# A decoder kernel: the last batch's block feed-forward and second norm spread over ten passes of the second self-attention

## What is computed

```python
# x = x + _L0_ffn_ref(_layernorm(x), weight, bias, delta_w, delta_act)      (the block feed-forward)
xb = x.reshape(-1, 32)                          # blocks of 32
amax = max(abs(xb)); e = floor(log2(max(amax, TINY)))
scale = exp2(e - 2.0) * exp2(0.5 * tanh(4 * delta))
xs = xb / scale
q = sign(xs) * _fp4_round(clip(abs(xs), 0.0, 6.0))
y = scale * q;  out = y @ w_q.T + bias

# x = x + _L1_attn_ref(_layernorm(x), ...)                                   (the second self-attention)
q, k, v = split(x @ W_attn.T + b_attn)          # 16 heads of 16 columns
att = q @ k.T / sqrt(16) + rel_bias;  att = softmax(where(causal, att, -inf))
y = (att @ v) @ W_proj.T + b_proj
```

## Time and profile before

| | us |
|---|---|
| median of 3 runs | 1368.73 (1368.17 to 1368.84) |
| the profiled execution | 1369.26 |
| its span, at a mean granted clock of 0.972 | 1367.5 |
| TensorE busy in the span | 1242.6 (91%) |
| VectorE busy | 1004.1 (73%) |
| ScalarE busy | 771.3 (56%) |
| GpSimd busy | 250.3 (18%) |
| the loop of the second self-attention | 1004.47 to about 1135.2 |

### The profile page before, as it was taken

One profiled execution on the slowest core, in us unless ns is written; L12 is line 12 of the kernel. 1 busy time (PEld: TensorE's weight loads), 2 busy tenths in 40 slices (PEclk: granted clock), 3 DMA queues, 4 the chain that ended last, 5 costly groups with the idle time before them and its releaser, 6 DMA issues.

```text
span 1367.5 us, 27670 instructions
## 1 busy us (share of the span) xinstructions
PE 1242.6 (91%) x9826; PEld 1064.5 (78%) x9826; DVE 1004.1 (73%) x2487; ACT 771.3 (56%) x1797; POOL 250.3 (18%) x338
## 2 busy tenths in 40 slices
PE   5999999979999999999999999999889999979638
PEld 5899999968788777878778787777667777769628
DVE  5976787656677777777777777777677995775975
ACT  5554545364655556555555555565545764425996
POOL 2433333342000000000000000000034454210100
PEclk9999999989999999999999999999999999989859
DMA  9200010131000000000000000000020003310001
GB/s 285 74 1 22 27 36 12 51 118 38 12 9 4 12 13 11 11 1 10 12 11 12 11 0 12 11 0 1 1 62 2 3 2 113 108 31 0 1 1 48
DMA packets 34547, 40.65 MB, mean 30 GB/s; under 512 B 4889, under 2 KB 29066, under 8 KB 34442
## 3 DMA queue, kind: packets, MB, share of 16 engines
q1 hardware_dynamic: 33614, 39.24, 9.5%
q10 hardware_dynamic: 828, 0.14, 0.1%
HBM read 35.36 MB, written 4.01 MB: 29 GB/s over the span
## 4 chain that ended last, share of the span: by engine, by line
PE 50%; DVE 16%; ACT 7%; issue 6%; POOL 1%; DVEq 0%; ACTq 0%; POOLq 0%
PE bank L796 8%; PE bank L798 7%; PE bank L797 7%; PE bank L1022 4%; PE bank L1012 3%; PE bank L1004 3%; PE bank L980 3%; ACT prob L1704 2%; DVE nmx L2403 2%; PE bank L1259 2%; PE bank L1277 2%; DVE kTl L2174 2%; DVE amax L2602 2%; PE bank L1396 2%; PE bank L1354 1%
## 5 line engine op out<-in xcount | busy, mean ns | idle before, releaser
L1704 ACT ACTIVATE prob<-bank,nmx 100x361 f32<-100x361 f32 x256 | 142.6, 560 | 203.4 <-DVE nmx L2403 197.0
L2403 DVE TENSOR_REDUCE nmx<-bank 100x1 f32<-100x361 f32 x256 | 124.1, 526 | 62.6 <-PE bank L1004 61.5
L700 POOL TENSOR_TENSOR frstd<-fmoments,eps 100x1 f32<-100x1 f32 x32 | 6.2, 194 | 644.2 <-DVE fmoments L2346 644.2
L796 PE MATMUL bank<-cxTh,wxkh 128*128 128x362 f32 x256 | 99.9, 390 | 9.4 <-DVE kTl L2174 8.2
L2420 DVE TENSOR_SCALAR prob<-prob,rsum 100x361 f32<-100x361 f32 x256 | 92.9, 405 | 4.5
L1012 PE MATMUL bank<-ident,prob 100*128 100x100 f32 (+1 forms) x768 | 89.1, 251 | 2.2 <-DVE prob L2420 2.1
L1012 PEld LDWEIGHTS bank<-ident,prob 100*128 100x128 f32 (+1 forms) x768 | 84.1, 150 | 7.6 <-DVE prob L2420 3.4
L796 PE MATMUL bank<-wxvh,cxTh 128*128 128x512 f32 (+1 forms) x192 | 84.5, 440 | 2.3 <-DVE vv L2326 2.1
L798 PE MATMUL bank<-cxTh,wxkl 128*128 128x362 f32 x256 | 84.1, 329 | 0.0
L797 PE MATMUL bank<-cxTl,wxkh 128*128 128x362 f32 x256 | 83.8, 327 | 0.0
L1022 PE MATMUL bank<-pT,vv 128*64 128x100 f32 (+1 forms) x1536 | 80.5, 253 | 1.7 <-ACT pT L1698 0.6
(11 more groups left out here) (436 smaller groups left out, 3711.2 us busy)
## 6 DMA issues: line engine op xcount, KB each, us to landing
cx<-in_ctx_dram SPq DMA_DIRECT2D x32, 128.0 KB, 2.1
xc<-in_ctx_dram SPq DMA_DIRECT2D x32, 128.0 KB
parked_weights<-parking SPq DMA_DIRECT2D x9, 256.0 KB, 5.6
mask_i<-in_mask_BxS_ik_dram SPq DMA_DIRECT2D x16, 141.0 KB
w<-in_L_attn_W_dram SPq DMA_DIRECT2D x2, 1024.0 KB, 13.8
cx<-in_ctx_dram SPq DMA_DIRECT2D x16, 105.0 KB, 2.0
xc<-in_ctx_dram SPq DMA_DIRECT2D x16, 105.0 KB
x<-in_x_dram SPq DMA_DIRECT2D x4, 400.0 KB
```

The costliest lines, as they stand in the source:

```text
L796: pe.matmul(o, wh, mh, start=start, stop=False)
L1704: nc.scalar.activation(prob[:, h % 4, :], bank[S_BANKS[e]][0:T, 0:S], ACT.Exp, bias=nmx[:, h:h + 1], accum_out=psum_[:, h:h + 1]).then_inc ...
L2403: nc.vector.tensor_reduce(nmx[:, h:h + 1], bank[S_BANKS[e]][0:T, 0:S], AX_X, ALU.max, negate=True).then_inc(xa_max, 1)
```

## The change

Batch 15's feed-forward and second norm are taken out of passes 0 to 2 and placed one piece at a time: on VectorE `blocks_scaled` behind pass 2's scores, `blocks_clipped` behind pass 4's, `blocks_quantised` behind pass 5's, the product's addition and the moments behind pass 7's, `row_normalised` into pass 9 behind `heads_scaled`. On TensorE the block transposes come in pass 6, the product in pass 7 and the row transposes in pass 9, each behind the fourth group of heads and a wait for ScalarE's copy of the third group (`a1_ca`), and each into bank 4 (`bank[TB[0]]`) in place of bank 7. Three new waits at the heads of passes 7, 8 and 10 keep bank 4 until it has been read; the waits that guarded bank 7 in passes 0 to 2 are gone. ScalarE's two copies follow in passes 6 and 9; GpSimd's `rstd_of` comes in pass 8 and `row_with_bias` in pass 10. No instruction is added or removed. The diff without the parts in which functions only get the bank as a parameter:

```diff
@@ GpSimd
-                if b == 1:
+                if b == 8:
                     rstd_of(2 * B, 1)
+                if b == 10:
                     row_with_bias(B - 1)
...
@@ TensorE
-            def both_transposes(src):
+            def both_transposes(src, o):
 
                 for k in range(KD):
-                    mm = pe.transpose(bank[W_BANK][:, k * T:(k + 1) * T], src[:, k * P:(k + 1) * P], ident[0:T, 0:T])
+                    mm = pe.transpose(o[:, k * T:(k + 1) * T], src[:, k * P:(k + 1) * P], ident[0:T, 0:T])
                 mm.then_inc(ff_t, 1)
...
@@ keys_projected
+                if i == PAIRS - 1:
+                    pe.wait_ge(ff_c, 2 * B)
...
@@ queries_projected
-                if i == 2:
-                    pe.wait_ge(ff_c, 2 * B)
...
+            LAST_BLOCK = {6: block_transposes, 7: block_product, 9: row_transposes_2}
             for b in range(B):
                 if b + 1 < B:
                     head_scores(b + 1)
+                if b == 7:
+                    pe.wait_ge(ff_c, 2 * B - 1)
+                if b == 8:
+                    pe.wait_ge(ff_x, B)
+                if b == 10:
+                    pe.wait_ge(ff_c, 2 * B)
                 heads_transposed(b, 0)
                 heads_transposed(b, 1)
-                if b == 1:
-                    pe.wait_ge(ff_x, B)
                 if b:
                     heads_output(b - 1)
                 heads_transposed(b, 2)
                 heads_transposed(b, 3)
-                if b == 0:
-                    pe.wait_ge(a1_qb, 2)
-                    block_transposes(B - 1)
-                if b == 2:
-                    pe.wait_ge(a1_x, 2)
-                    row_transposes_2(B - 1)
+                if b in LAST_BLOCK:
+                    pe.wait_ge(a1_ca, 4 * b + 3)
+                    LAST_BLOCK[b](B - 1, bank[TB[0]])
...
                 heads_weighted(b)
-                if b == 0:
-                    block_product(B - 1)
...
@@ ScalarE
-                if b == 0:
-                    blocks_copied(B - 1)
-                if b == 2:
-                    rows_copied(B - 1, zT[:, PAIRS - 1, :, T:])
+                if b == 6:
+                    blocks_copied(B - 1, bank[TB[0]])
+                if b == 9:
+                    rows_copied(B - 1, zT[:, PAIRS - 1, :, T:], bank[TB[0]])
...
@@ VectorE
-                if b == 1:
-                    block_product_added(B - 1)
-                    row_moments(B - 1, 1)
-                if b == 2:
+                if b == 9:
                     row_normalised(B - 1)
                 if b + 1 < B:
                     values_out(b + 1)
-                if b == 0:
-                    blocks_scaled(B - 1)
-                    blocks_clipped()
-                    blocks_quantised(B - 1)
                 if b + 1 < B:
                     scores_out(b + 1)
+                if b == 2:
+                    blocks_scaled(B - 1)
+                if b == 4:
+                    blocks_clipped()
+                if b == 5:
+                    blocks_quantised(B - 1)
+                if b == 7:
+                    block_product_added(B - 1, bank[TB[0]])
+                    row_moments(B - 1, 1)
```

More of the change, by code:

```diff
@@ L1036, in block_transposes, with block_product, row_transposes_2 @@
                     pe.wait_ge(ff_c, 2 * j)
-                both_transposes(fq)
-            def block_product(j):
+                both_transposes(fq, o)
+            def block_product(j, o=bank[W_BANK]):
                 pe.wait_ge(ff_c, 2 * j + 1)
                 for k in range(KD):
-                    mm = pe.matmul(bank[W_BANK][0:T, 0:D], fqT[:, k, :], wffn[:, k, :], start=(k == 0), stop=(k == KD - 1))
+                    mm = pe.matmul(o[0:T, 0:D], fqT[:, k, :], wffn[:, k, :], start=(k == 0), stop=(k == KD - 1))
                 mm.then_inc(ff_mm, 1)
-            def row_transposes_2(j):
+            def row_transposes_2(j, o=bank[W_BANK]):
                 pe.wait_ge(ff_q, 2 * j + 2)
-                both_transposes(z_row)
+                both_transposes(z_row, o)
             def mirrored(j):
@@ L1705, in exponent, with blocks_copied, rows_copied @@
                                      accum_out=psum_[:, h:h + 1]).then_inc(xa_exp, 1)
-            def blocks_copied(j):
+            def blocks_copied(j, o=bank[W_BANK]):
                 act.wait_ge(ff_t, 2 * j + 1)
-                nc.scalar.copy(fqT[:], bank[W_BANK][:, 0:KD * T].rearrange("d (k q) -> d k q", k=KD)).then_inc(ff_c, 1)
-            def rows_copied(j, dst):
+                nc.scalar.copy(fqT[:], o[:, 0:KD * T].rearrange("d (k q) -> d k q", k=KD)).then_inc(ff_c, 1)
+            def rows_copied(j, dst, o=bank[W_BANK]):
                 act.wait_ge(ff_t, 2 * j + 2)
-                nc.scalar.copy(dst, bank[W_BANK][:, 0:KD * T].rearrange("d (k q) -> d k q", k=KD)).then_inc(ff_c, 1)
+                nc.scalar.copy(dst, o[:, 0:KD * T].rearrange("d (k q) -> d k q", k=KD)).then_inc(ff_c, 1)
             def mirror_copied(j):
@@ L2370, in blocks_quantised, with block_product_added @@
                 nc.vector.tensor_tensor(blocks(fq[:]), blocks(fa[:]), over(fscale[:], 8), ALU.mult).then_inc(ff_q, 1)
-            def block_product_added(j):
+            def block_product_added(j, o=bank[W_BANK]):
                 dve.wait_ge(ff_mm, j + 1)
-                link(nc.vector.tensor_tensor(row(j), bank[W_BANK][0:T, 0:D], row(j), ALU.add))
+                link(nc.vector.tensor_tensor(row(j), o[0:T, 0:D], row(j), ALU.add))
                 nc.vector.tensor_tensor(row(j), row(j), bffn[:], ALU.add).then_inc(ff_x, 1)
```

2 lines of the change are left out of this document (1 added, 1 removed).

## The result

The changed kernel takes 1372.72 us, the median of 20 runs (1366.51 to 1375.17), beside 1370.31 for 20 runs of before (1368.17 to 1372.36). The ratio is 1.0014, 95% interval 1.0007 to 1.002. The forecast was 1366.7 with a range up to 1370.3, so it missed: by the interval the change costs 1 to 3 us where it was to bring 2. The profiled execution took 1373.56 us (span 1371.7) against 1369.26 (1367.5), 4.3 us more.

A forecast was written before the change was run, and what follows sets the result against it. TensorE was taken to set the pace from pass 3, with excess in passes 0 and 2 from the last batch's feed-forward; -10.2 + 0.7 + 3.4 + 2.1 + 2.0 = -2.0 us gave 1366.7 us, range 1363.8 to 1370.3.

The forecast's parts named there:

- the first term of the sum: Passes 0 to 2: removing the last batch's feed-forward shortens them from 33.8 to 23.6 us, -10.2 us.
- the +0.7 for the clock: Pass 0's value product and the following scores may run at half clock: +0.7 us, bounds 0 and 1.7.
- The insertions: Moved work arriving in later passes: +3.4 us on VectorE, +2.1 from GpSimd's interference, +2.0 on TensorE.
- the new gaps: Passes 3, 5 and 6: TensorE waits 1.6, 1.6 and 1.9 us for the values.
- +3.4: VectorE in later passes: moved steps exceed its idle cover in passes 2, 4, 5 and 9, +3.4 us.
- +2.1: Passes 2, 4 and 5: GpSimd's subtractions stall VectorE's moved steps, +2.1 us, bounds 0 and 3.5.
- +2.0: TensorE: waits and transposes add 0.4 us each in passes 6 and 9, wait and product 1.15 in pass 7.
- The holds: VectorE's moved steps stand still during GpSimd's subtractions, until some 0.15 us before GpSimd's recorded end.
- both rivals on them: GpSimd doesn't stall VectorE: 1364.6 us, chance 0.21; or stalls it to GpSimd's recorded end: 1367.4 us, chance 0.10.
- One fall: TensorE's clock falls once in the waits of passes 3, 5 and 6: +1.4 us, 1370.1 us, chance 0.15.
- two or more: TensorE's clock falls at least twice in the waits of passes 3, 5 and 6: +4.8 us, 1373.5, chance 0.08.
- a clock below 1.00 in these passes: Sign that the prediction is wrong: granted clock below 1.00 between passes 3 and 10.

The follow-up runs named there:

- the second profile of before: The unchanged kernel run again with a profile of its own: 1370.58 us, ratio 0.9999.
- after: The changed kernel itself, against the unchanged one: 1372.72 us, ratio 1.0014.
- the filling: The changed kernel with 14, 14 and 16 unread dummy transposes on TensorE in the waits of passes 3, 5 and 6: 1370.05 us, ratio 1.0000.
- the second measurement of after: The changed kernel run once more without alteration, twelve runs: 1372.27 us, ratio 1.0004 to the unchanged kernel.
- one-line version: The unchanged kernel with only GpSimd's last-row bias moved behind pass 3's subtractions, measured twice: 1365.49 us (0.9961) and 1364.73 us (0.9964).
- the last version above: Version with quantising in its old place, plus the normalised row at pass 8's end and GpSimd's root in pass 7: 1367.61 us, ratio 0.9981.

## Why the prediction was wrong

**In short.** The step that failed is the first term of the sum: 10.2 us freed in passes 0 to 2, 9.5 with the +0.7 for the clock. It was read from one execution with a low stretch in pass 2. Measured were 8.1 us against that profile and 6.2 against the second profile of before. The insertions came out as forecast (7.6 us against 7.5), and -6.2 + 7.6 = +1.4 is near what the means of the runs show. The falls of the clock in the new gaps, which the sum left out, come on top in both profiles of after, but not in every execution.

**Right: the steps at full clock.** The gaps were 1.68, 1.72 and 1.99 us (1.6, 1.6, 1.9 forecast), the additions on TensorE +0.5 in pass 6 (where there is no gap: 8.01 - 7.52), +1.25 in pass 7 and +0.9 in pass 9 with the normalised row (0.4, 1.15 and 0.75). Passes 3 to 9 take 63.4 us against 52.4, and without the two low stretches, at half of their length, 1.7 us each, the rise is 7.6 (7.9 by the 1.6 and 1.5 that the filling won back); the terms +3.4, +2.1 and +2.0 make 7.5. The holds exist and end 0.14 us ahead of GpSimd's record, which sets both rivals on them aside. TensorE didn't wait at the heads of passes 7, 8 and 10.

**Wrong first: the term of -10.2 us.** I took passes 0 to 2 from one profile, 33.8 us. In it pass 2 has a low stretch of 6.8 us; another profile of the same kernel has none and 31.9 us. So 1.9 us of the 10.2 were an execution's, not the kernel's, and measured against that profile passes 0 to 2 give 6.2. A row of one execution that holds a low stretch is not the cost of the code.

**Wrong next: +0.7 for the start.** The low stretch there is 10.2 us, where I had gone on from the 6.8 of the earlier trace rows. Passes 0 and 1 take 18.2 us against the forecast's 16.8: 1.4 us more. It also begins sooner, 1.8 us after the pass's start in place of 4.2, so the transposes run at half clock too. With 6.8 us of it, in the profile with the filled gaps, the same two passes take 16.7, so the 1.4 are the length of that execution's low stretch, which isn't the code's either.

**Wrong last: the clock in the gaps.** "One fall" had a chance of 0.15 and "two or more" of 0.08, and both profiles of after have two. The prediction had named a clock below 1.00 in these passes as a sign against it. The evidence that I set against it was one gap of 1.38 us with a steady clock; that the clock fell 1.8 us behind the gap of 2.54 in pass 2 of the same trace I hadn't weighed. The size was off too: I priced a fall at 3.4 us from a stretch of 6.8, and each stretch was 3.4 us long and cost 1.5 to 1.6. So it is luck that the rival's 1373.5 us lie close to the measured 1372.72: it has too much for the falls and, in its -10.2, too much for the gain. Within the loop the errors close: -2.0 forecast, +1.4 for the start, +3.1 for two falls and +0.4 for the insertions make +2.9, and +3.0 was measured against the first profile.

**In the runs.** The mean clock of the 104 runs of before whose clock is known is 0.9709 and of 32 runs of after 0.9708: 79.6 and 80.1 us of low time. Between sets of before's runs it lies from 0.9704 to 0.9719, so this can't tell 1 us of time; taken beside each other, in the second measurement of after, it is 0.9707 for before and 0.9709 for after. On the average over executions the change neither gives nor takes clock that could be seen. I had put 6.8 us of low time, 3.4 us, on the gain's side. The sum without it is -2.0 + 3.4 = +1.4. If half of the low time is taken off the loop, the two profiles of before give 108.5 and 108.4 and those of after 109.8 and 109.9: +1.4. The measured means are 1370.30 and 1371.86: +1.6. That these three agree doesn't show that each part is right, since half of a low stretch is too much at the loop's start; it bounds the share of the clock.

**What the term lumped together.** The -10.2 us stand for all that leaves passes 0 to 2, and the prediction didn't ask which part of it has to leave. The version with the quantising in the old place shows that VectorE's time is free there, to 0.1 us: what must go is TensorE's waiting for the quantised row and GpSimd's for the normalised one. The latter alone is worth 4.7 and 5.3 us by the medians (ratios 0.9961 and 0.9964) and costs nothing that shows in the later passes, as the added bias has its first reader at the loop's end. In passes 0 to 2 it frees 3.4 and 3.7 us (28.5 and 28.2 against 31.9), where the large change frees 6.2 and pays 7.6 us of insertions. More than half of what it frees is to be had by one line.

**Open.** What takes the clock down. The length of a gap alone doesn't decide: it fell behind 1.68, 1.99, 2.28 and, once of twice, 2.54 us, and not behind 1.72 us, nor 1.66 in pass 8 of the last version above. In what share of the executions each falls isn't known, with one or two profiles of each kernel. Why the runs of after scatter more (1366.1 to 1375.2) than those of most versions is put down to this, by the clock, but the falls of single executions were not seen. Of the one-line version's 4.7 and 5.3 us, 3.4 and 3.7 are seen in passes 0 to 2; its mean clock is 0.9718 and 0.9730 beside before's 0.9710 and 0.9719, which is 2.3 and 3.0 us less of low time, up to 1.1 and 1.5 us more. That this is the low stretch of pass 2, which one of two profiles of before has, agrees with it and wasn't shown.

## What to carry to other kernels

Look for the queue before moving work: an engine that waits in order for a late input (GpSimd, 7 us) holds everything behind it, and moving that one instruction can be worth more than spreading a whole block. Work moved into a loop that TensorE bounds must be cut to the idle time of its engine, here 0.6 us a pass, with the hold by GpSimd counted; beyond it, each piece costs its excess at once, and the clock can fall besides. Take a baseline with low clock in it from two profiles at least, and keep the clock's part of a sum apart.

## What the runs showed of the hardware

- Gaps of TensorE of 1.68 and 1.99 us in an otherwise full stretch were each followed by 3.4 us at half clock in two of two profiles, one of 1.72 by none; with 14 and 16 dummy transposes in them the clock stayed at 1.00 in the one profile taken and the passes lost 1.6 and 1.5 us. A gap of 2.54 us in the same code was followed by 6.8 us at half clock in one execution and by none in another.
- A low stretch in unchanged code ahead of the loop was 0, 3.4, twice 3.4 or 10.2 us long from one execution to another.
- A scaling with its factors read per partition (line 2352, one wide input) is stretched by GpSimd as the two-input steps are: 0.69 us where a subtraction was under way when it began (pass 2 of after), 0.40 where it began 0.10 us ahead of one (1005.60 in the earlier trace rows); there the subtraction took 1.01 us in place of 0.85.
- With VectorE setting the end at the loop's start, filling TensorE's waits there went with 6.8 us less of low time, by the mean clock, and changed the time by 0.3 us, within what the runs can tell.
